# Convolution work in another order, and a third buffer for gathered target rows, in a graph network on one core

## The reference, cut to what matters

```python
def gat(x, src, dst):                       # 8 heads of 32
    h = x @ W
    e = leaky_relu(a_src(h)[src] + a_dst(h)[dst], 0.2)
    alpha = segment_softmax(e, dst)
    return relu(segment_sum(h[src] * alpha, dst) + bias)

def convs(x, src, dst):                     # 3 layers
    for l in range(3):
        xi, xj = x[src], x[dst]
        e = relu((xj - xi) @ thetas[l].T + xi @ phis[l].T)
        agg = segment_max(e, src)           # nodes without an edge: 0
        x = relu(batchnorm(agg) * gammas[l] + betas[l])
    return x

x = layernorm(x + gat(x, (src, dst)))
x = layernorm(x + convs(x, src, dst))
```

## Time and profile before

| what | us |
|---|---|
| median of the timed runs | 1758.32 |
| the profiled execution, its own time | 1768.92 |
| its span, first to last instruction | 1767.1 |
| PE busy | 1076.6 (61%) |
| DVE busy | 1239.4 (70%) |
| ACT busy | 985.7 (56%) |
| POOL busy | 955.6 (54%) |
| chain that ended last | PE 42%, DMA 20%, DVE 20%, issue 6%, POOL 5%, ACT 4% |

### The profile page before, as it was taken

The page is one execution under the profiler, slowest core; times in us unless marked ns, Lnnn a source line. Parts: engine busy times, 40 slices in busy tenths (PEclk is TensorE's granted clock), DMA queues, the critical chain, the costliest instruction groups (busy, mean ns, idle before and its releaser), DMA issues.

```text
span 1767.1 us, 16600 instructions
## 1 busy us (share of the span) xinstructions
PE 1076.6 (61%) x3823; PEld 562.5 (32%) x3823; DVE 1239.4 (70%) x2657; ACT 985.7 (56%) x2630; POOL 955.6 (54%) x1013
## 2 busy tenths in 40 slices
PE   0139888781004661699999699997999987000000
PEld 0023333330002331455555355554545544000000
DVE  8847877678978994255455355563666678989998
ACT  4735877665455775244444455564555453766665
POOL 1047756667767777777777677524544137640000
PEclk9999999895557876799999899998999999555555
DMA  9276899988694674588886589856866359999999
GB/s 366 101 227 214 284 324 354 334 306 257 222 294 157 202 228 144 155 261 264 255 269 203 120 187 202 184 162 122 153 141 134 84 186 309 420 412 389 383 404 366
DMA packets 174965, 431.98 MB, mean 244 GB/s; under 512 B 28308, under 2 KB 107682, under 8 KB 154900
## 3 DMA queue, kind: packets, MB, share of 16 engines
q1 hardware_dynamic: 107748, 227.24, 37.0%
q0 software_dynamic: 43904, 98.91, 22.9%
q10 hardware_dynamic: 23216, 104.77, 16.8%
HBM read 254.11 MB, written 180.72 MB: 246 GB/s over the span
## 4 chain that ended last, share of the span: by engine, by line
PE 42%; DMA 20%; DVE 20%; issue 6%; POOL 5%; ACT 4%; SPq 2%; ACTq 0%; POOLq 0%; DVEq 0%
PE ps L1296 14%; PE ps L1309 14%; DMA out<-arena 10%; PE ps L1286 4%; DMA arena<-x 3%; DMA x_dst<-arena 3%; DVE stat L806 2%; PE ps L1473 2%; PE ps L1325 2%; PE ps L887 2%; DMA arena<-x,idx 2%; POOL x L1162 2%; ACT arena L845 2%; DVE arena L1068 2%; DVE arena L803 2%
## 5 line engine op out<-in xcount | busy, mean ns | idle before, releaser
L1381 DVE TENSOR_TENSOR_SCAN arena<-arena,ps 128x512 f32<-128x512 f32 (+1 forms) x150 | 186.7, 1253 | 242.5 <-PE ps L1296 209.2
L860 POOL DMA_INDIRECT arena<-x,idx x196 | 186.1, 949 | 182.5 <-DVE idx L622 90.8
L1267 POOL DMA_INDIRECT arena<-agg,slot x196 | 185.3, 945 | 181.4 <-PE ps L1286 80.4
L1309 PE MATMUL ps<-arena 128*128 128x512 f32 x600 | 269.5, 592 | 10.5 <-ACT arena L1351 10.5
L1296 PE MATMUL ps<-arena 128*128 128x512 f32 x600 | 270.1, 593 | 0.0
L1242 POOL DMA_INDIRECT arena<-x,idx x196 | 185.6, 947 | 61.0 <-issue 57.0
L1578 ACT ACTIVATE ps<-arena 128x256 f32<-128x256 f32 x391 | 143.7, 367 | 96.4 <-DVE arena L1550 96.4
L845 ACT ACTIVATE arena<-arena,shift,inv 128x256 f32<-128x256 f32 (+1 forms) x311 | 156.1, 589 | 50.9 <-DVE shift L837 34.2
L1385 DVE TENSOR_TENSOR ps<-arena,ps 128x512 f32<-128x512 f32 (+1 forms) x150 | 101.7, 683 | 96.6 <-PE ps L1309 96.3
L1351 ACT ACTIVATE arena<-big,bn_shift,bn_scale 128x512 f32<-128x512 f32 (+1 forms) x100 | 75.1, 798 | 162.1 <-PE ps L1309 150.3
L1309 PEld LDWEIGHTS ps<-arena 128*128 128x128 f32 x600 | 115.5, 193 | 151.5 <-issue 139.9
(11 more groups left out here) (214 smaller groups left out, 2166.9 us busy)
## 6 DMA issues: line engine op xcount, KB each, us to landing
arena<-x SPq DMA_DIRECT2D x39, 1280.0 KB, 9.3
out<-arena SPq DMA_DIRECT2D x39, 1280.0 KB, 11.8
arena<-x ACTq DMA_DIRECT2D x31, 1280.0 KB, 10.5
x<-arena ACTq DMA_DIRECT2D x31, 1280.0 KB, 6.4
agg<-arena SPq DMA_DIRECT2D x48, 512.0 KB, 4.1
arena<-not_same SPq DMA_DIRECT2D x72, 256.0 KB
arena<-last_of SPq DMA_DIRECT2D x72, 256.0 KB
x_dst<-arena SPq DMA_DIRECT2D x24, 512.0 KB, 3.6
```

What stands on the lines that cost most here:

```text
L860: pl.indirect_dma_start(rows_in[:, par, a, g, :], None, x[:, :], bass.IndirectOffsetOnAxis(ap=idx[:, k, t * G + g:t * G + g + 1], axis=0)) ...
L1267: pl.indirect_dma_start(conv_in[:, b, 1, g, :], None, agg_dram[l - 1][:, :], bass.IndirectOffsetOnAxis(ap=slot[:, t * G + g:t * G + g + 1] ...
L1309: m = pe.matmul(near_bank[j][:, 0:width(t)], thp[:, l, 1, k, j * P:(j + 1) * P], near_t[:, par, k, 0:width(t)], start=(k == 0), stop=(k == 1))
L1381: v.tensor_tensor_scan(runmax[:, par, j, 0:width(t)], mask[:, tl % 2, 0:width(t)], far_bank[j][:, 0:width(t)], initial, ALU.add, ALU.max). ...
```

## The change

It has these parts.

* Attention stage: the dst rows get a ring of three buffers (`DST_RING`, the third being `rows_dst_3`); the src rows keep two. POOL's dst gathers of tile t now wait for the store and the transposes of tile t - 3, its src gathers for tile t - 2 as before. To make room in SBUF, `msq` and `tiles_f` now lie inside `score`.
* Convolution 0 on PE: the step is split in halves: far transposes of t, near product of t - 1, near transposes of t, rows of t - 2, far product of t. `keep_rows` on ACT and `store` on SP come one step earlier (two behind instead of three).
* Convolutions 1 and 2 on PE: after the first transposes the far product of tile 0 follows at once, then tile 1, before tile 2 is transposed; the later steps are as they were. Nine matmuls whose result nobody reads (`keep_clock`) stand around the first near product.
* SP: in every step the masks are issued before the store, and at a layer's end the last stores stand together ahead of the last masks.
* ACT: `keep_rows` of the last tile stands before the squares of the last tile.

```diff
@@ gat_pool
-                if t > 1:
-                    pl.wait_ge(s_row_turned, 4 * (t - 1))
-                    pl.wait_ge(s_xd_stored[par], 16 * (t // 2))
-                for a, k, got in ((1, D_DST, s_dst_got), (0, D_SRC, s_src_got)):
-                    for g in range(cols(t)):
-                        pl.indirect_dma_start(rows_in[:, par, a, g, :], None, x[:, :], ...
+                if t >= DST_RING:
+                    pl.wait_ge(s_row_turned, 4 * (t - DST_RING) + 2)
+                    pl.wait_ge(s_xd_stored[t % DST_RING], 16 * (t // DST_RING))
+                for g in range(cols(t)):
+                    pl.indirect_dma_start(dst_rows(t)[:, g, :], None, x[:, :], ...
+                if t > 1:
+                    pl.wait_ge(s_row_turned, 4 * (t - 1))
+                for g in range(cols(t)):
+                    pl.indirect_dma_start(src_rows(t)[:, g, :], None, x[:, :], ...
@@ conv_sync
-            first = 2 if l else 0
-            for s in range(first, NS + 3):
-                if l < L - 1 and 0 <= s - 3:
-                    store(s - 3)
-                if s < (NS + 2 if l < L - 1 else NS):
-                    masks(s)
+            lag = 2 if l == 0 else 3
+            for s in range(2 if l else 0, NS):
+                masks(s)
+                if l < L - 1 and s >= lag:
+                    store(s - lag)
             if l < L - 1:
+                masks(NS)
+                for t in range(NS - lag, NS):
+                    store(t)
+                masks(NS + 1)
@@ conv_pe
+            def keep_clock(count):
+                pe.wait_ge(s_conv_scan, 2 * NS * l)
+                for _ in range(count):
+                    pe.matmul(far_bank[0], ident[:, :], thp[:, l, 0, :, :].rearrange("p k f -> p (k f)"), start=True, stop=True)
-            if l:
-                near(0)
-            in_steps([(0, turn), (1, products)] + ([(2, rows)] if l < L - 1 else []), NS)
+            if l == 0:
+                for t in range(NS):
+                    turn(t, False)
+                    if t > 0:
+                        near(t - 1)
+                    turn(t, True)
+                    if t > 1:
+                        rows(t - 2)
+                    far(t)
+                near(NS - 1)
+                rows(NS - 2)
+                rows(NS - 1)
+                return
+            keep_clock(4)
+            near(0)
+            keep_clock(5)
+            turn(0, False)
+            far(0)
+            turn(1, False)
+            far(1)
+            near(1)
+            for s in range(2, NS + 2):
+                if s < NS:
+                    turn(s, False)
+                if 2 < s <= NS:
+                    far(s - 1)
+                    near(s - 1)
+                if l < L - 1:
+                    rows(s - 2)
@@ conv_act
-            in_steps([(0, keep)] + ([(3, keep_rows)] if l < L - 1 else []) + [(2, squares)], NS)
+            for s in range(NS + 2):
+                if s < NS:
+                    keep(s)
+                if l == 0 and s >= 2:
+                    keep_rows(s - 2)
+                if l == 1 and s >= 3:
+                    keep_rows(s - 3)
+                if l == 1 and s == NS + 1:
+                    keep_rows(NS - 1)
+                if s >= 2:
+                    squares(s - 2)
...
```

More of the change, by code:

```diff
@@ L154, in gnn @@
         s_src_got = [sem("src_got_0"), sem("src_got_1")]
-        s_dst_got = [sem("dst_got_0"), sem("dst_got_1")]
+        DST_RING = 3
+        s_dst_got = [sem(f"dst_got_{b}") for b in range(DST_RING)]
         s_row_turned = sem("row_turned")
         s_row_kept = sem("row_kept")
-        s_xd_stored = [sem("xd_stored_0"), sem("xd_stored_1")]
+        s_xd_stored = [sem(f"xd_stored_{b}") for b in range(DST_RING)]
         s_logits = sem("logits")
@@ L869, in turn @@
                     a, j = 1 - n // 2, n % 2
-                    if j == 0:
-                        pe.wait_ge((s_src_got, s_dst_got)[a][t % 2], 16 * cols_landed(t, 2))
+                    if n == 0:
+                        pe.wait_ge(s_dst_got[t % DST_RING], 16 * cols_landed(t, DST_RING))
+                    if n == 2:
+                        pe.wait_ge(s_src_got[t % 2], 16 * cols_landed(t, 2))
+                    rows = dst_rows(t) if a else src_rows(t)
                     if t:
@@ L874, in turn @@
                     for g in range(cols(t)):
[L875 removed]
+                        m = pe.transpose(bank[n][:, g * P:(g + 1) * P], rows[:, g, j * P:(j + 1) * P], ident[:, :])
                     m.then_inc(s_row_turned, 1)
@@ L957, in soft_in_sync @@
                 sp.wait_ge(s_score_stored[par], 16 * (NS // 2 + 1 - par))
-            for par in range(2):
-                sp.wait_ge(s_xd_stored[par], 16 * (NS // 2 + 1 - par))
+            for b in range(DST_RING):
+                sp.wait_ge(s_xd_stored[b], 16 * len(range(b, NS, DST_RING)))
             sp.dma_start(sc, score_dram.rearrange("h (b q) -> (h b) q", q=BQ)).then_inc(s_scores_in, 16)
@@ L1273, in conv_pe, with turn @@
                 pe.wait_ge(s_x1_sum, NC)
-            def turn(t):
+            def turn(t, near_rows):
                 b = t % RC
-                pe.wait_ge(s_far_got[b], 16 * far_landed(l, t))
-                for n in range(4 if l == 0 else 2):
+                if near_rows:
+                    pe.wait_ge(s_near_got[b], 16 * cols_landed(t, RC))
+                else:
+                    pe.wait_ge(s_far_got[b], 16 * far_landed(l, t))
+                for n in (2, 3) if near_rows else (0, 1):
                     a, j = 1 - n // 2, n % 2
-                    if n == 2:
-                        pe.wait_ge(s_near_got[b], 16 * cols_landed(t, RC))
                     use = turns_before(l, t) + n
@@ L1310, in near @@
                     m.then_inc(s_near_done, 1)
-            def products(t):
-                far(t)
-                if l == 0 or t:
-                    near(t)
+            def keep_clock(count):
+                pe.wait_ge(s_conv_scan, 2 * NS * l)
+                for _ in range(count):
+                    pe.matmul(far_bank[0], ident[:, :], thp[:, l, 0, :, :].rearrange("p k f -> p (k f)"), start=True, stop=True)
             def rows(t):
```

36 lines of the change are left out of this document (21 added, 15 removed).

## The result

The changed kernel takes 1754.1 us (median, 1751.16 to 1763.3, 17 runs). The kernel before, run beside it, took 1768.15 (1753.51 to 1777.27, 17 runs). The ratio is 0.9938, 95% interval 0.9919 to 0.9957, so about 11 us faster (8 to 14); a second comparison gave 0.9938 again (0.9916 to 0.9961). The forecast was 1739, range 1726 to 1750: the direction was right, and the time lies 4 us above the range. The profiled execution took 1751.16 us, with a span of 1749.3.

A forecast was written before the change was run, and what follows sets the result against it. Taken as bounds: attention's PE-DVE-ACT loop, then DMA (0.95 busy); PE in convolution 0, POOL's gathers close behind; PE in convolutions 1 and 2. Gains 9 + 5.5 + 1 + 4 = 19.5 us off 1758.3 gave 1739, range 1726 to 1750.

The forecast's parts named there:

- part 6: Start of convolution 2: earlier store 1.0 us, far product of tile 2 sooner after the first gather 3; gain 4.
- Part 1: Start of the attention stage: POOL's first store wait goes and the loop starts earlier; gain 2.0 us, bounds 0 and 5.95.
- Part 2: Attention, 240 to 390 us: POOL's six store waits go, DMA then limits; gain 5 us, at most 7.5.
- Part 3: From the attention loop to convolution 0: its first gather starts 9 us earlier; bounds 2 and 23.
- loop's 7: Attention stage: the two-tile loop ends 7 us earlier, and DVE and ACT carry this on to convolution 0.
- Part 4: Convolution 0: PE becomes bound by gathers, POOL's lookups bound the hand-over to convolution 1; gain 5.5 us, bounds 3 and 7.5.
- Part 5: Start of convolution 1: far product of tile 2 sooner after the first gather; gain 1.0 us, bounds 2 and minus 2.
- third buffer hidden: Rival, 19%: in the attention stage DMA is full, the third buffer gives nothing; only the convolutions' 10.5 us remain, 1748.
- loads of dense groups displaced: Rival, 5%: at DVE's bias add, 250 to 410 us, extra gathers delay dense loads; 32 us slower, 1780 in all.
- Gathers set free: Rival, 12%: mid-attention DMA isn't the limit, the stage falls to the loop's pace; sum 33.5 us, 1725.
- Both small: Rival, 9%: third buffer gives nothing, layer starts lose their gains to the slow clock; 2.5 us, 1756.

## Why the prediction was right and wrong

Two steps failed: the base on which the gain was laid, and the 3 us for the start of conv 2 in part 6.

**The base.** The forecast was laid on the median of three runs, 1758.3 us, though the profiled execution took 1768.92. Four comparisons put before at 1768.15, 1764.6, 1763.41 and 1762.02 us, the first of them with those three runs among its 17. The unrounded forecast is 1738.8, and 1754.1 is 15.3 above it. In the comparison that measured the change, 9.8 of these 15.3 us are the base (1768.15 less 1758.32); by the other three it would be 4 to 6. The other 5.5 are the gain: 19.5 forecast, 14.05 between the medians (11 by the ratio). The step that failed was "The median of the timed runs is 10.6 us (0.6%) lower than the profiled one; the parts are small enough not to be scaled", which took three runs as the kernel's time. Their own spread, 1757.24 to 1765.64, was nearly half the forecast gain.

**Part 1** (2.0, start of the attention): right in its mechanism, too small in its size. PE's wait of 2.05 us is gone, and POOL's too. But the logits behind that wait had run slowly, 5.02 us at a granted clock of 0.71, and now take 3.60 at 1.00. The sum had no term for this. DVE's eleventh copy of scores begins 4.2 us earlier (235.9 to 231.7); in the mean of four profiles with two buffers and five with three it is 3.0.

**Part 2** (5, 240 to 390 us): the waits for `x_dst` went, but for 1.0 us. The last copy of scores comes 8.1 us earlier (402.3 to 394.2), where parts 1 and 2 had 7; 4.2 of it were there by 240 us, so part 2 gave about 4 in this pair, and 6.5 in the mean of the same nine profiles, around its 5. What was late next was not shown to be the DMA alone, as the prediction had it: POOL now waits for PE (15.3 us) and DVE for loads (21.0 us). The cap of 7.5, worked out from the idle 0.05 of the DMA, was not passed, but it takes a busy share for a rate, and at the same share of 0.96 the DMA moved 344 and then 351 GB/s. The Trainium skill says in "DMA: Bandwidth & Descriptors", section "Issuing engines are not separate DMA queues", that DMAs of all issuing engines run on the same 16 DMA engines and interleave. The prediction took from it that the buffer buys no bandwidth; the trace agrees to within those 2%, and the freed 20 us didn't come.

**Part 3** (first gather of conv 0 9 earlier): 12.7 in the pair of profiles, 12.3 over all. POOL does now wait for ACT (9 waits, at most 1.5 us), which the prediction named as the limit. The term that was too small is the "loop's 7": ACT normalizes tiles 20 and 21 at 664.25 instead of 675.20, 10.9 us earlier. POOL used 1.8 of the 2.6 us that ACT had to spare. Of the 10.9 us 8.1 were there at the last copy of scores, and all of them at the last store of a dense group (543.1 to 531.6 us). No run shows what gave the rest in between.

**Part 4** (5.5): right, 5.4 over all profiles, and by the named mechanism. PE's waits for ACT in conv 0 (8.0 us) are gone, and it waits for gathers instead, though in 9 steps and not in each. POOL comes out of its lookups and waits 2.19 us for the last to land (2.2 forecast). Two of the inner numbers were off and cancelled out of the sum. The last rows end 17.3 us behind POOL's last gather (952.70 less 935.4), not 13, so they came nearer by 9.2, not by 12 to 13. The prediction hung 8 to 9 us of work on the last gather's landing, but PE had 16.0 us of work without a wait for gathers behind the one of tile 23 (936.74 to 952.70). The loss behind the lookups is therefore 6, not 9: with 8 lookups fewer there, the hand-over came 6.1 us earlier and then waited for SP.

**Part 5** (1.0): far of tile 2 came at 28.3 against 29.2 forecast and 30.2 before; a little better than said.

**Part 6** (4) is the step that failed among the terms. The first 1.0, the earlier store, is there and is 1.5: last rows to first gather took 6.55 us and takes 5.05 (the masks ahead of the store took 1.49). The 3 became minus 1.5, so the part was 4.5 us too large. The prediction named the mechanism, "holds up the first transposes by up to 8", but only for a filler at the slow clock, and put it at nothing in the sum. The filler ran at the full clock (4.45 us for its five matmuls, granted clock 1.00) and held them up all the same: it stood behind near, which was slow (6.05 us, granted clock 0.61), and in front of the transposes, which began at 1203.82, 13.0 us behind the first gather instead of 8.1. Without the filler far of tile 2 is at 26.8 against the forecast 25.5, and to the last scan it takes 199.5 us: 2.5 us were the filler's. Of the 3 us forecast the order alone gave 1.0.

The Trainium skill says in "TensorE: Matmul & The Clock Gate", section "HAM oscillation — how this bites in real kernels", that idle gaps between bursts of matmuls bring PE back to the half rate. The trace agrees: near runs slowly behind 4.46 us of idle time. The prediction took from it that the filler would save one slow product in conv 2; it came behind that product and saved none.

**Timed and profiled.** For the third buffer the profiles give 12.3 us at the first gather of conv 0, its timed comparison 6.2 (2 to 10). The profiled run was often among the faster of its kernel (1744.17 against a median of 1752.3 for the changed kernel run again, 1753.32 against 1757.4 for the third buffer alone), but not for the kernels without filler (1748.59 against 1747.27). What follows the last scan can take back one of the other 6 us; whether the rest is luck of the profiled runs or is lost again in timed ones stays open. So it also stays open why the parts, 18.7 us in the profiles, are worth 11 to 14 in timed runs. That they come so near to the 19.5 forecast is in part luck: part 3 gave 3.3 more than said, and part 6 4.5 less.

Of the rivals, "third buffer hidden" and "loads of dense groups displaced" are refuted by the third buffer alone (0.9944 to 0.9987). DVE's waits for loads did grow, to 21.0 us, but stayed short (3.4 at most). The effect of the whole, 11 us by the ratio, lies nearest to the first of the two in size, for other reasons. "Gathers set free" would have had conv 0 start 23 us earlier; it was 12 to 13. "Both small" falls with the third buffer alone and with part 4, though its parts 5 and 6 did come to nothing in the timed runs.

## What to carry to other kernels

Lay a forecast on the kernel's time only as firmly as its runs agree: where three runs spread over 8 us, the time after a gain of 11 to 14 can't be laid on their median, and a profile far from their median is a sign that they are not the whole picture. Filler on an in-order engine must stand where the real work behind it can't be ready: price it as a wait in the sum, with the time from its end to the arrival of the next operand. And when a hand-over is bound by leftover work on the gathering engine, moving that work pays only if it isn't put between the first gathers of the next stage: twelve lookups ahead instead of 20 were worth nothing with the rest from tile 2 on, and some 5 to 6 us with the rest from tile 6 on.

## What the hardware showed

A far product in conv 1 ran at 5.36 us (granted clock 0.69), although five filler matmuls and transposes at the quick rate (1.09 us for eight) stood just before it, with 1.60 and 1.10 us idle between (the rows from 964.92 on). In the second profile of the changed kernel the same product took 6.77 us (0.54), behind 2.66 and 1.10 us idle. In conv 2, with no idle time between the filler and the transposes, it ran at 3.70 (1.00). But the filler is not what decides: with the lookups from tile 6 on, and no filler, the same product of conv 1 ran at 3.70 (1.00) behind a slow near (5.63), 1.54 us idle, the same quick transposes and 1.10 us idle. No run settles what made the difference.

The same DMA share of 0.96 went with 344 and with 351 GB/s. And the same kernel took 1762 to 1765 us on three chips and 2092 on a fourth: there 30 us were to be had from an order of conv 0 that gave 4 to 6 elsewhere, since POOL waited for stores of `x_src` that never held it on the others.
